# Expanding the heads' maxima of an attention stage with one maximum over an axis of length one instead of two copies

## What is computed

```
dots = jnp.einsum('bhnd,bhmd->bhnm', q, k)
attn_grass = jnp.einsum('bhnd,bhmd->bhnm', qgr, kgr) ** 2 * grassman_scale
a = jnp.concatenate([dots * scale, dots ** 2 * riem_scale, attn_grass], axis=1)
a = ... batch norm over the 24 maps ...
a = jnp.einsum('oc,bcnm->bonm', conv_w, a) + conv_b[None, :, None, None]
a = jax.nn.softmax(a, axis=-1)
out = jnp.einsum('bhnm,bhmd->bhnd', a, v)
```

## Time and profile before

| | us |
|---|---|
| median of 3 runs | 1054.82 |
| lowest and highest run | 1050.14, 1056.47 |
| the profiled execution's own time | 1052.94 |
| its span | 1051.3 |
| TensorE busy in the span | 846.5 (81%) |
| VectorE busy in the span | 776.8 (74%) |
| GpSimd busy in the span | 506.2 (48%) |
| ScalarE busy in the span | 452.2 (43%) |

### The profile page before, as it was taken

How to read it: one execution, slowest core, us unless ns; L and a number is a source line. 1 busy time by engine, 2 the same in 40 slices (tenths; PEclk the granted TensorE clock), 3 DMA queues, 4 the chain that set the end, 5 groups by cost and what they waited for, 6 DMA issues and landing times. The chain is left out here.

```text
span 1051.3 us, 40125 instructions
## 1 busy us (share of the span) xinstructions
PE 846.5 (81%) x16806; PEld 611.4 (58%) x16806; DVE 776.8 (74%) x1227; ACT 452.2 (43%) x966; POOL 506.2 (48%) x551
## 2 busy tenths in 40 slices
PE   3677578998938888888888888888888888789995
PEld 2233245555536666666766667666766676646663
DVE  4588954887967878778787777877778877647773
ACT  1333422115514444444444444444444444447774
POOL 3456621110036666667566665766656666412220
PEclk9888888998959989989899998999989989869998
DMA  8665000224011111111111111111111111001111
GB/s 305 244 230 177 1 0 18 54 52 123 1 35 54 54 53 53 39 51 54 44 48 51 54 54 36 54 54 54 45 44 54 54 50 40 19 0 30 29 29 32
DMA packets 64293, 64.92 MB, mean 62 GB/s; under 512 B 36825, under 2 KB 54812, under 8 KB 64156
## 3 DMA queue, kind: packets, MB, share of 16 engines
q1 hardware_dynamic: 63628, 61.24, 18.8%
q10 hardware_dynamic: 528, 1.54, 0.4%
HBM read 52.93 MB, written 6.75 MB: 57 GB/s over the span
## 5 line engine op out<-in xcount | busy, mean ns | idle before, releaser
L1165 ACT ACTIVATE sq<-ps_dot 128x376 f32<-128x376 f32 x384 | 165.0, 482 | 191.0 <-PE ps_dot L1064 191.0
L997 POOL TENSOR_TENSOR v_blk<-v_rep,vmask 128x384 f32<-128x384 f32 x128 | 106.5, 853 | 153.7 <-PE ps_m L1095 153.7
L1064 PE MATMUL ps_dot<-q_st,k_blk 64*64 64x94 f32 x6144 | 171.8, 250 | 0.9 <-ACT sq L1165 0.6
L1064 PEld LDWEIGHTS ps_dot<-q_st,k_blk 64*64 64x64 f32 x6144 | 135.9, 135 | 54.7 <-issue 32.7
L1159 ACT ACTIVATE prob<-prob,head_const 128x376 f32<-128x376 f32 x128 | 78.0, 609 | 155.0 <-DVE prob L1213 155.0
L1203 DVE COPY row_max_e<-row_max_o 94x128 f32<-94x128 f32 x128 | 122.7, 1025 | 2.2
L1188 DVE TENSOR_REDUCE row_max<-ps_a 128x94 f32<-128x564 f32 x128 | 89.5, 740 | 29.8 <-PE ps_a L1115 29.8
L1077 PE MATMUL ps_a<-ident,row_max_e 94*128 94x94 f32 x128 | 26.6, 293 | 102.6 <-DVE row_max_e L1203 102.6
L1012 POOL TENSOR_TENSOR half<-prob 128x564 f32<-128x564 f32 x64 | 75.5, 1180 | 62.7 <-ACT prob L1160 62.7
L1019 POOL TENSOR_TENSOR k_blk<-k_cm,hmask 128x768 f32<-128x768 f32 x64 | 96.8, 1513 | 1.8 <-PE ps_a L1107 1.8
L1088 PE MATMUL ps_m<-prob,v_blk 128*64 128x94 f32 x1536 | 96.4, 287 | 1.2 <-DVE q_cm L1220 1.2
(11 more groups left out here) (225 smaller groups left out, 1472.7 us busy)
## 6 DMA issues: line engine op xcount, KB each, us to landing
v_rep<-v_rows SPq DMA_DIRECT2D x128, 192.0 KB, 3.0
x_g<-in_x_dram SPq DMA_DIRECT2D x15, 1500.0 KB, 6.8
v_rows<-tok SPq DMA_DIRECT2D x16, 192.0 KB
q_st<-q_cm SPq DMA_DIRECT2D x64, 47.0 KB, 1.8
out_dram<-rows SPq DMA_DIRECT2D x16, 188.0 KB
x_g<-in_x_dram ACTq DMA_DIRECT2D x1, 1500.0 KB, 7.4
top_rows<-tok SPq DMA_DIRECT2D x16, 32.0 KB
top<-top_rows SPq DMA_DIRECT2D x1, 512.0 KB, 3.5
```

The lines of the kernel that those rows point to most:

```text
L997: vb = pool.tensor_tensor(v_blk[:, a, b].rearrange("p t (o d) -> p (t o) d", o=H), v_rep[:, a, b].rearrange("p (t o d) -> p (t o) d", o=H, ...
L1064: mm = pe.matmul(ps_dot[64 * v:64 * v + 64, (2 * g + b) % 3, N * c:N * c + N], k_blk[rows, a, SLOTS * (3 * v + g) + c].rearrange("p k h m ...
L1165: act.activation(sq[:, b, :, g, :], ps_dot[:, (2 * g + b) % 3, 0:SLOTS * N].rearrange("p (c n) -> p c n", c=SLOTS), ACT.Square).then_inc(s ...
```

## The change

In `heads_max`, two copies, one for each batch, become one `tensor_reduce` for both. The copies read the 8 heads of one batch and write them 16 times (the source has a stride of zero over x); the first writes with the heads outermost, x innermost. The reduction takes the maximum over a last axis that is added and has length one, so it passes each value through unchanged; it reads both batches, writes `top_e` in the order in which it lies in memory (batch, x, head), 256 results per partition, and raises the same semaphore. The waits before and after stay, and so does everything else.

```diff
                 dve.wait_ge(s["max_heads"], prev + 1)
-                for b in range(2):
-                    spread = dve.tensor_copy(top_e[:, b].rearrange("n x o -> n o x"), top_o[:, b].unsqueeze(2).broadcast_to([N, H, 16]))
-                spread.then_inc(s["max_ready"], 1)
+                dve.tensor_reduce(top_e[:], top_o[:].unsqueeze(2).unsqueeze(4).broadcast_to([N, 2, 16, H, 1]), AX.X, ALU.max).then_inc(s["max_ready"], 1)
```

## The result

| | before | after |
|---|---|---|
| median, us | 1055.11 (4 runs) | 920.32 (4 runs) |
| lowest and highest, us | 1050.14, 1056.47 | 919.02, 921.80 |
| the profiled execution's own time, us | 1052.94 | 921.80 |
| its span, us | 1051.3 | 920.1 |

The ratio is 0.873, with an interval of 0.870 to 0.876: 13% faster. The forecast was 927.8 us in a range from 918 to 950.

The account below looks back on a forecast made before the run. TensorE's wait for the `heads_max` copies bounds the attention stage. Removing 96 us of wait and 31 us of half-rate stretches takes 1052.94 to 925.9 us; 1.9 us for the runs' median gives 927.8 us, range 918 to 950.

Parts of the forecast that it names:

- What bounds: Attention stage: TensorE sets the pace and idles 102.6 us in total, waiting for the two copies of `heads_max`.
- Why the copies were slow: Copies in `heads_max`: each waits until a GpSimd instruction ends, 2.00 us a pair against 0.42 us where GpSimd is idle.
- The new reduction: Expansion in `heads_max`: one reduction of 256 elements takes 0.42 us; lower bound 0.27 us, upper bound 1.22 us.
- Does it wait for GpSimd: New reduction in `heads_max`: no wait, since the reductions at L468 beside GpSimd stay between 917 and 937 ns.
- The new step: Attention stage: 7.27 us without wait plus 0.10 us of wait left is 7.37 us, in 60 steps.
- The clock: TensorE in the attention stage: full clock in all 60 steps, as the longest idle stretch shrinks from 1.68 to 0.10 us.
- The other engines: Attention step of 7.37 us: GpSimd busy 6.16 us, ready 0.41 us before its value blocks; VectorE 5.88, ScalarE 4.38.
- A (clock): Attention stage: the clock still falls in as many steps, 31 us come back, 959 us; chance 0.05.
- B (dear group): New reduction: a group of one is dear, 1.22 us, total 977 us (0.04); middle case 944 us (0.09, shared with C).
- C (next bound): Attention steps: GpSimd's margin or VectorE's latencies are smaller, 16 us more, 944 us; chance 0.09, shared with B's middle case.
- D (price of a result): New reduction: each result costs 7.9 ns, 2.17 us in all, total 1071 us; chance 0.03 together with its twin.
- D's twin: New reduction: held by GpSimd to the same end as the copies, saves nothing, about 1055 us; chance 0.03 together with D.

Follow-up runs that it names:

- the copies in order: Kernel before, its two copies with the 16 groups outermost and the heads innermost, so writing in the order of memory: 1060.97 us, ratio 1.008.
- four reductions: Changed kernel with the expanding reduction issued four times, the extra ones into a tile that nobody reads: 985.38 us, ratio 0.936.

## Why the prediction was right, point by point

*What bounds.* Right: TensorE's wait for the expansion was on the path in every step. All of it, and its consequences, came off the total.

*Why the copies were slow.* Right, and shown from three sides: a copy ends a constant distance behind a GpSimd instruction (in the trace of before, 124 of the 128 copies end 0.13 to 0.14 us behind one; the other four lie where GpSimd has nothing to do), follows that instruction when it is made shorter, and a two-input operation in its place is held as well. What I had not seen is that one copy for both batches would have got most of the gain, 118 of some 135 us.

*The new reduction.* Taken at 0.42 us, measured at 0.416. The reasoning was incomplete, though. I argued from the number of results per input and left out the order of the elements, which the change also altered; that the figure came out right is in this part luck. With the old order the same reduction takes 0.61 us and the total would have been 933 us. That is inside my range, but for a reason that I had not named.

*Does it wait for GpSimd.* No, as forecast; 415 to 417 ns.

*The new step.* Forecast 7.37 us, measured 7.36. The 0.10 us of wait that I had left in it is there, but not where I had looked for it: I had put near 6 us in total for TensorE's idle time before L1077, and the profile gives 1.0 us, all of it in the last step, and no idle time for waits as short as the others.

*The clock.* Forecast 1.00 throughout, measured 1.00. The cause that I read from the rows, the idle stretch, holds in the run that makes as long a wait without any copy.

*The other engines.* They fit. GpSimd kept 0.3 to 0.4 us of spare time ahead of its value blocks, as worked out. A few intervals of 7.4 to 7.9 us (six of them, 0.06 to 0.54 us longer than the rest, 1.6 us in all) belong to none of my terms. In the two longest the time is lost within the 48 matmuls of the linear part, 1.63 and 1.48 us from their start to that of the squares instead of 1.08, at full clock and with no releaser named; the cause is open.

*The sum.* The forecast lies 7.5 us above the measurement. In the stage itself it was 592.61 - 127.0 = 465.6 us against 464.96. The term that was wrong in it is the first interval, 9.47 us before: I took 0.80 us off, and it became 7.15 us, because a part of it had run at low clock too (the 48 matmuls of the linear part took 1.92 us there and 1.15 in a usual step, the 32 of the squares 2.11 and 1.28); the odd intervals just named gave most of this back. The rest lies outside the stage. Its start moved from 318.75 to 317.93 us. Behind it, the span went on for 139.9 us before (911.36 to 1051.3) and for 137.2 after (782.89 to 920.1), where I had kept it fixed. The expert block's stretch shows why:

```profile
783.40:919.80 136.40, 118.05 (x618) 76.37 (x618) 81.34 (x104) 79.79 (x181) 26.94 (x65) 0.92 0.10 23
```

The same 618 matmuls, 118.05 us busy instead of 121.07, at clock 0.92 instead of 0.89. Nothing of the change reaches this stage's own work, and why its clock differs was not settled. From the last reduction of the heads to the end it is 137.1 to 137.3 us in all three traces of the changed kernel, but 139.8 with the copies in order and 140.9 with four reductions, whose `finish` is the same. So it differs between kernels by up to 3.7 us while the changed kernel repeats it within 0.2 us, and I had left no room for that in the sum. Finally I had added 1.9 us because the profiled execution of before was below its median; the one of after was 1.5 us above, which makes 3.4 us. 0.6 + 0.8 + 2.7 + 3.4 = 7.5 us.

*The rivals.* A (clock), B (dear group), C (next bound) and D (price of a result) all fell. D's twin, a reduction that is held like a copy, is refuted by its spread of 2 ns.

## What to carry to other kernels

When a tiny VectorE operation takes far longer than its elements and its durations spread widely, look at what GpSimd does at its end: if the end follows a GpSimd instruction at a constant distance, the operation is being held, and one that is not held (here a reduction over an axis of length one) or fewer, better placed instructions remove the wait. Price such a wait on TensorE from its own steps at both clocks: one of 1.07 us cost only itself, one of 1.6 to 1.7 us cost nearly as much again (1.55 us) in a third to three quarters of the steps. When one instruction is replaced by another, compare every difference between them, also the order in which they read and write: here it was worth 11 us by itself. And before crediting the new operation, try the new count with the old one: either alone removed most of this wait.

## What the runs showed that I had not expected

- A reduction of 256 elements to 256 results on 94 partitions takes 416 ns when it writes in the order of memory and 611 ns when it writes with steps of 8 elements (and reads each input 16 times in a row).
- A copy that gets in between two GpSimd instructions lengthens the one behind it, 1.57 us instead of 1.51.
- The number of steps in which TensorE's clock falls does not follow the length of the wait: about 20, 28 and 48 intervals at waits of 1.68, 1.62 and 1.72 us.
- Four matmuls of the attended values by themselves hold TensorE for 0.31 us, while 24 in one piece take 1.03 us.
- The stage behind the change, with the same work, lasted 137.1 to 140.9 us from kernel to kernel, and the same within 0.2 us in the three traces of the changed one.
